# A causal mask added in the bank by VectorE, in place of products with an identity

## The reference, cut to what matters

```python
kv_c = x @ W_kv
kv_c = kv_c * jax.lax.rsqrt(jnp.mean(kv_c * kv_c, axis=-1, keepdims=True) + EPS) * g_kv
q_c = x @ W_q
k_content = heads(kv_c @ W_kdec, HEAD_DIM)
v = heads(kv_c @ W_vdec, HEAD_DIM)
q_content = heads(q_c @ W_qdec, HEAD_DIM)
k_rope = heads(x @ W_krope, ROPE_DIM)
q_rope = heads(q_c @ W_qrope, ROPE_DIM)
cos, sin = _rope_tables(Tx, ROPE_DIM)
q_rope = _apply_rope(q_rope, cos, sin)
k_rope = _apply_rope(k_rope, cos, sin)
q = jnp.concatenate([q_content, q_rope], axis=-1)
k = jnp.concatenate([k_content, k_rope], axis=-1)
scale = 1.0 / jnp.sqrt(jnp.float32(q.shape[-1]))
scores = jnp.einsum('bhqd,bhkd->bhqk', q, k) * scale
causal = jnp.tril(jnp.ones((Tx, Tx), dtype=bool))
scores = jnp.where(causal[None, None], scores, jnp.float32(-jnp.inf))
attn = jax.nn.softmax(scores, axis=-1)
out = jnp.einsum('bhqk,bhkd->bhqd', attn, v)
return out @ W_o
```

## Time and profile before

| what | us |
|---|---|
| median of 3 runs | 9698.33 |
| lowest, highest run | 9677.0, 9698.8 |
| the profiled execution | 9704.18 |
| its span | 9702.4 |
| TensorE busy with products | 6747.6 (70%) |
| VectorE busy | 4783.5 (49%) |
| ScalarE busy | 3123.7 (32%) |
| GpSimd busy | 2120.6 (22%) |

### The profile page before, as it was taken

The page is one execution under the profiler, slowest core; times in us unless marked ns, Lnnn a source line. Parts: engine busy times, 40 slices in busy tenths (PEclk is TensorE's granted clock), DMA queues, the critical chain, the costliest instruction groups (busy, mean ns, idle before and its releaser), DMA issues. The chain is left out here.

```text
span 9702.4 us, 109745 instructions
## 1 busy us (share of the span) xinstructions
PE 6747.6 (70%) x36480; PEld 3514.7 (36%) x36480; DVE 4783.5 (49%) x7251; ACT 3123.7 (32%) x6809; POOL 2120.6 (22%) x2322
## 2 busy tenths in 40 slices
PE   5766755667756577655546999877677666677777
PEld 4666541411244112211112444434344333344343
DVE  4555424246423465477774444444444555444444
ACT  2111123235412255133331122344344333344343
POOL 1222120221132311034431100033142000033231
PEclk7788776768878688777778687988888777788888
DMA  0000010122111110000000322111110000011110
GB/s 28 0 0 0 19 44 21 44 66 61 47 45 54 41 35 24 11 0 0 0 0 13 63 49 45 34 39 33 32 36 21 7 0 0 16 36 31 36 36 25
DMA packets 249853, 264.30 MB, mean 27 GB/s; under 512 B 111392, under 2 KB 178848, under 8 KB 247520
## 3 DMA queue, kind: packets, MB, share of 16 engines
q1 hardware_dynamic: 241248, 242.23, 9.5%
q0 software_dynamic: 8192, 16.79, 0.6%
HBM read 122.56 MB, written 69.21 MB: 20 GB/s over the span
## 5 line engine op out<-in xcount | busy, mean ns | idle before, releaser
L1781 ACT ACTIVATE s_l3l_probs<-ps,s_l3l_biases,s_l3l_q_inverse 128x128 f32<-128x128 f32 x1024 | 454.8, 454 | 630.5 <-DVE s_l3l_biases L1846 630.5
L2005 PE MATMUL ps<-s_l2b_hc,ident 128*128 128x512 f32 x512 | 355.2, 832 | 407.8 <-DVE s_l2b_hc L2097 407.6
L1972 POOL TENSOR_TENSOR s_l2b_Bx<-s_l2b_du,s_l2b_B 128x512 f32<-128x512 f32 x256 | 415.2, 1645 | 620.4 <-DVE s_l2b_du L2085 375.2
L2092 DVE TENSOR_TENSOR_SCAN s_l2b_state<-s_l2b_decay,s_l2b_Bx 128x512 f32<-128x512 f32 x256 | 430.6, 1720 | 114.4 <-POOL s_l2b_Bx L1972 114.4
L592 DVE TENSOR_REDUCE s_L1a_negmax<-ps 128x1 f32<-128x512 f32 x512 | 324.8, 684 | 192.5 <-PE ps L460 188.5
L1010 DVE TENSOR_REDUCE s_L3a_negmax<-ps 128x1 f32<-128x128 f32 (+3 forms) x512 | 236.1, 488 | 349.6 <-PE ps L846 346.9
L592 DVE TENSOR_REDUCE s_L2a_negmax<-ps 128x1 f32<-128x512 f32 x512 | 324.2, 684 | 151.4 <-PE ps L460 148.5
L1632 POOL TENSOR_TENSOR s_l3l_probs<-s_l3l_probs,s_l3l_inverse 128x512 f32<-128x512 f32 x256 | 265.9, 1039 | 572.1 <-DVE s_l3l_inverse L1851 563.3
L1654 PE MATMUL ps<-s_l3l_hs,s_l3l_wqk 128*128 128x512 f32 x512 | 308.4, 723 | 114.7 <-POOL s_l3l_hs L1600 70.8
L861 PE MATMUL ps<-s_L3a_ks,s_L3a_qs 40*128 40x256 f32 (+3 forms) x1024 | 355.3, 600 | 29.0 <-DVE s_L3a_kvsq L1025 16.5
L988 ACT ACTIVATE s_L3a_pt<-ps 128x256 f32<-128x256 f32 (+3 forms) x512 | 195.4, 434 | 520.5 <-PE ps L846 518.6
(11 more groups left out here) (658 smaller groups left out, 16214.4 us busy)
## 6 DMA issues: line engine op xcount, KB each, us to landing
s_l3l_qk<-s_l3l_rope SPq DMA_DIRECT2D x1024, 64.0 KB, 2.0
scratch_rope<-s_L3a_rope SPq DMA_DIRECT2D x32, 512.0 KB, 2.8
s_L3a_qs<-scratch_rope SPq DMA_DIRECT2D x64, 128.0 KB
s_L3a_ks<-scratch_rope SPq DMA_DIRECT2D x64, 128.0 KB
s_L0e_slots<-scratch_sent SPq DMA_DIRECT2D x16, 384.0 KB, 5.7
scratch_done<-s_L0e_back SPq DMA_DIRECT2D x48, 128.0 KB, 1.7
scratch_square<-s_L1a_rows SPq DMA_DIRECT2D x24, 256.0 KB
scratch_parts<-s_L1a_split SPq DMA_DIRECT2D x16, 384.0 KB
```

The costliest lines, as they stand in the source:

```text
L1781: act.activation(t["probs"][:, U % (LAG + 1), k, :], ps[:, U % 2, P * k:P * (k + 1)], ACT.Exp, bias=t["biases"][:, U % (LAG + 1), k:k + 1] ...
L1972: pool.tensor_tensor(t["Bx"][:, n % 2, k, :], t["du"][:, k, :], t["B"][:, n % 2, :], ALU.mult).then_inc(s["bx_ready"], 1)
L2005: pe.matmul(ps[:, 4 + k, :], g["ident"][:, :], t["hc"][:, (n - 1) % 2, k, :], start=(n == 1), stop=(n == STATES)).then_inc(s["summed"], 1)
L2092: vec.tensor_tensor_scan(t["state"][:, k, :], t["decay"][:, n % 2, k, :], t["Bx"][:, n % 2, k, :], 0.0, ALU.mult, ALU.add).then_inc(s["sca ...
```

## The change

The two products of `masked` are left out for the maxima and for the turned scores. VectorE adds the mask in the bank instead. The table of masks is now two float32 tables of 128 columns (no identity, no bfloat16 copy). A new function `hide` waits for the scores' product (`scored`), adds the turned mask to the 128 diagonal columns of each of the pair's two banks and then signals `turned_ready` to ScalarE; `maxima` adds its mask to the last 128 columns, waits for that addition (`masked`), and then reduces. GpSimd's cast goes.

```diff
-               "wqrope": ([64, 4, P], F32), "wo": ([P, P], F32), "cos": ([P, T], F32), "sin": ([P, T], F32), "masks": ([P, 2, 3, P], F32), "masksb": ([P, 2, 3, P], BF16),
+               "wqrope": ([64, 4, P], F32), "wo": ([P, P], F32), "cos": ([P, T], F32), "sin": ([P, T], F32), "masks": ([P, 2, P], F32),
...
-            own(pool.tensor_copy(t["masksb"][:, :, :, :], t["masks"][:, :, :, :]))
...
-            def masked(out, r, kind):
-
-                for j in range(2):
-                    mm = pe.matmul(out, t["masksb"][64 * r:64 * r + 64, j, 0, :], t["masksb"][64 * r:64 * r + 64, j, kind, :], start=False, stop=(j == 1))
-                return mm
-
...
-                    pe.matmul(out[:, 0:(qt + 1) * P], t["qs"][rows, b % 2, n // 2, qt * P:(qt + 1) * P], t["ks"][rows, b % 2, n // 2, 0:(qt + 1) * P], start=True, stop=False)
-                    mm = masked(out[:, qt * P:(qt + 1) * P], n % 2, 1)
+                    mm = pe.matmul(out[:, 0:(qt + 1) * P], t["qs"][rows, b % 2, n // 2, qt * P:(qt + 1) * P], t["ks"][rows, b % 2, n // 2, 0:(qt + 1) * P], start=True, stop=True)
...
-                              start=True, stop=False)
-                for r in range(2):
-                    masked(ps[:, 2 * pair + r, kt * P:(kt + 1) * P], r, 2).then_inc(s["turned_ready"], 1)
+                              start=True, stop=True).then_inc(s["scored"], 1)
...
+            def hide(b, u, pair):
+
+                kt = u % KT
+                for r in range(2):
+                    vec.wait_ge(s["scored"], START + 4 * (b * NH + u) + 2 * pair + r + 1)
+                    own_keys = ps[:, 2 * pair + r, kt * P:(kt + 1) * P]
+                    vec.tensor_tensor(own_keys, own_keys, t["masks"][:, 1, :], ALU.add).then_inc(s["turned_ready"], 1)
+
...
+                    own_keys = out[:, qt * P:(qt + 1) * P]
+                    vec.tensor_tensor(own_keys, own_keys, t["masks"][:, 0, :], ALU.add).then_inc(s["masked"], 1)
+                    vec.wait_ge(s["masked"], START + (b * HALVES + n // 2) * 2 * KT + 2 * qt + n % 2 + 1)
                     taken_by(vec.tensor_reduce(t["negmax"][:, qt, n:n + 1], out[:, 0:(qt + 1) * P], AX.X, ALU.max, negate=True), item)
...
                     for half in range(2):
+                        hide(b, u, half)
                         if b + 1 < BATCH:
                             maxima(b + 1, 2 * u + half)
```

More of the change, by code:

```diff
@@ L733, in rotary_attention @@
     signals = ("loaded pool_ready ready6 ready7 taken6 taken7 squared rooted scaled rope_made nope_written rope_written0 rope_written1 first_stacked second_stacked max_written "
-               "max_stacked turned_ready exp_ready pv_done o_copied pool vec")
+               "max_stacked scored turned_ready masked exp_ready pv_done o_copied pool vec")
     with stage(nc, "L3a", tensors, signals) as (block, t, s):
@@ L2959, in layout @@
     later = np.where(np.arange(P)[None, :] > np.arange(P)[:, None], -1e30, 0.0)
-    rows = np.stack([np.eye(P), later, later.T], 1).reshape(2, 64, 3, P).transpose(1, 0, 2, 3)
-    o["L3a_masks"] = np.concatenate([rows, rows]).astype(np.float32)
+    o["L3a_masks"] = np.stack([later, later.T], 1).astype(np.float32)
     sel = np.zeros((P, 4, P), np.float32)
```

## The result

| | before | after |
|---|---|---|
| median, lowest, highest us | 9698.56, 9677.0, 9706.5 (4 runs) | 9851.49, 9847.2, 9862.0 (4 runs) |
| ratio | | 1.0163, 95% interval 1.0145 to 1.0181 |
| span of the profiled execution | 9702.4 | 9860.3 |
| this stage from its mark to the next | 960.7 | 1094.6 |

A forecast was written before the change was run, and what follows sets the result against it. TensorE's stream and its clock bound the stage. Six batches +60, seventh +10 in two terms of +5, eighth -1, first maxima +3, start -2: +70 us, forecast 9768, own range 9735 to 9825, wider range 9685 to 9890.

The forecast's parts named there:

- The bound: Six batches: TensorE's stream, busy 646 of 675.6 us; 1% more time at the lower clock costs about 0.5 us a batch.
- Part 1: TensorE: 2048 identity products go, saving 1.8 us in four steps at 2.4 GHz, 3.4 at 1.2; 7 and 13.5 a batch.
- Rival A: TensorE's stream alone decides and the additions hide: about -62 us, 9636; chance 0.12.
- Part 2: VectorE: 1024 additions of 128x128 in the bank come, 0.29 us each; VectorE goes from about 50 to 84 us a batch.
- Rival D: An addition on VectorE costs 0.48 us, VectorE past 100 us a batch at 2.4 GHz: about 9850; chance 0.06.
- Part 3: TensorE waits longer for the maxima's banks; net batch 92.2 to 99 us at 2.4 GHz, 162.6 to 157 at 1.2.
- B: Rival: waits come as worked out, the clock's share at 1.2 GHz stays 42%: about +34 us, 9732; chance 0.20.
- Part 4: TensorE's clock in the six batches: share at 1.2 GHz rises from 42% to 52%, a batch 122.6 us, +10.0.
- The sum: Six batches +60, seventh +5 and +5, eighth -1, first maxima +3, start -2: together +70 us, 9768; chance 0.45.
- C: Rival: clock stays low as in the first maxima, 80% of the time: about +190 us, 9888; chance 0.17.
- the signs that I listed for the forecast: Additions near 0.29, VectorE about 84 us a batch, batches 115 to 130 us, clock 0.70 to 0.77, first maxima 72 to 76.

The follow-up runs named there:

- square of four kernels: Mask products kept or dropped, VectorE additions absent or made: products only 9703.8, no products or additions 9708.3, both 9849.5, additions only (the changed kernel) 9851.5 us.
- the kernel with neither: Kernel before without the mask products and without VectorE additions, so no key is hidden: 9708.3 us, ratio 0.9997.
- the run in quarters: Kernel before, masks untouched, VectorE's two long reciprocals of a batch cut in quarters of 128 columns between later maxima: 9694.9 us, ratio 0.9975.

## Why the prediction was right or wrong

**The bound, right.** TensorE's stream sets the pace, and the clock is worth more than the edit: the square of four kernels shows it better than I had put it. By the forecast's own figures 1% more of the time at 1.2 GHz costs 0.6 us of a batch, not 0.5.

**Part 1, right in kind at a given clock, and worth nothing.** Without masks four steps at 1.2 GHz take 4.2 us less (24.9 for 29.1); I had 3.4. Step 2 at 2.4 GHz takes 0.28 less; a quarter of my 1.8 is 0.45. What I didn't see is that the share of time at 1.2 GHz moves against it. Rival A (-62) would have failed even with additions at no cost: the kernel with neither came to 9708, a ratio of 0.9997.

**Part 2, right.** 0.293 us an addition, 0.03 to the reduction, 82 us of VectorE in a batch. Rival D is out.

**Part 3, right at 2.4 GHz, too dear at 1.2.** The five steps seen whole at 2.4 GHz in both kernels take 31.5 us for 30.0, so a batch 96.8 where I had 99. The seven at 1.2 GHz take 47.9 for 52.8, so a batch 147.5 where I had 157. These steps stand for all: an estimate. At the old share the two cancel, 1/(0.57/96.8 + 0.43/147.5) = 113.6 us a batch for 113.3 by the same formula before, where B had +29 us in six.

**Part 4, the step that failed.** I put the share of time at 1.2 GHz at 52%; it is (1 - 0.66)/0.5 = 68% (0.64 in the second profile, 72%). With the measured paces 68% gives 126.3 us a batch, and 127.05 was measured; 52% would have given 117.9, about +32 us in six. So nearly all of the +86.7 is the share, and my +60 was that near only because Part 3 had the pace too dear: part of it is luck. The 52% came from the worst batch of before, a batch with before's queue on VectorE and all its mask products. I priced it by waits of TensorE behind VectorE. In the six batches the additions alone take the share from 43% to 50%, and the missing products alone to 64%. I had those as "10% of the products", without a price; they are 1537 of 4148 in the count, 37%, for some 8% of the time by Part 1. In the seventh batch it is the additions that bring the clock down. Whether the missing products do it as less work, or by the waits for a bank that they leave bare (16 us of the stage become 79), is open.

**The sum.** The seventh batch was mis-sized by the same step: +35 for my +10, since I gave it one fall and it was at 1.2 GHz for (1 - 0.61)/0.5 = 78% of the time. The eighth became 10 longer instead of 1 shorter, again by the clock (0.79). The first maxima, already at 0.50, came within about 1 us (+4.1 for +3), and the stage's start before them fell by some 2.5 us for my 2: where the clock can't fall, the working held.

**The rivals.** B's condition, the clock as it was, fails. C had the mechanism with a share of 80%; the truth, 68 to 72%, lies between forecast and C, and C's 9888 is nearer to 9851 than my 9768. Of the signs that I listed for the forecast the clock failed (0.66 for 0.70 to 0.77), and two of the six batches took 134.5 us, over the 130. I had said that the whole is wrong if other stages differ by more than 5 us. They differed by 24 in all in the first pair, and by 19 between two executions of the kernel before, so that test was set too fine.

## What to carry to other kernels

Where TensorE swings between its two clocks, work out a change at each level and then the share of time at each: here the same edit was about +5% and -9% on a batch at the two levels and +13% in truth. Taking products away bought nothing and lowered the clock. Putting an instruction of 0.29 us on a second engine behind each of 1024 products cost 146 to 153 us: alone, 98 us for the half in front of a bank's release and 34 for the half in front of the exponentials. Try such an edit by halves and as a square (old work kept, new work added, both, neither) before trusting a busy time. In each variant, look at the waits again, since an edit meant to change one thing (less work, another order) changed the waits as well in several of these runs. Profile the same code twice before reading a difference of ten microseconds.

## What the runs showed of the hardware

- Batches with the same instructions, one after the other, took 100.5 us at a clock of 0.92 and 128.6 at 0.71; 4.6 us of the difference are a wait for rows.
- An unchanged stage took 618.1 us at a clock of 0.84 in one execution and 652.1 at 0.77 in another of the same kernel.
- With all, half and none of the mask products the clock was 0.79, 0.75 and 0.68, and TensorE's waits for a bank 16.2, 43.6 and 78.8 us.
- VectorE adds 128x128 in a bank, reading and writing it, in 0.292 us; 128x16 takes 0.176. So 112 columns are worth 0.116 us, and by that some 0.16 is fixed (an estimate).
- A reciprocal of 128x128 takes 0.944 us in SBUF, 128x512 from a bank 3.358, by groups of the run in quarters:

```profile
L1060 DVE RECIPROCAL s_L3a_sums<-s_L3a_sums 128x128 f32<-128x128 f32 x28 | 26.4, 944 | 0.1
L1048 DVE RECIPROCAL s_L3a_sums<-ps 128x512 f32<-128x512 f32 x1 | 3.4, 3358 | 2.1 <-PE ps L898 2.1
```
